# The output projection of a state-space block in high and low parts, two pieces of the FFN later

## The reference, cut to what matters

```python
xz = einsum('bld,ed->ble', layernorm(x), in_proj_w)      # 256 -> 2 x 512
x_inner, z = split(xz, 2)
x_conv = silu(causal_conv_4_taps(x_inner) + conv_b)
x_dbl  = einsum('bld,ed->ble', x_conv, x_proj_w)         # delta, B, C
y = scan(h = h * exp(delta * A) + x_conv * delta * B; y = h . C)
y = (y + x_conv * D) * silu(z)
x = x + einsum('bld,od->blo', y, out_proj_w)             # 512 -> 256, the output projection
h = gelu(butterfly(layernorm(x) @ W_exp + b_exp) + up_bias)
x = x + butterfly(h) @ W_con + b_con + down_bias         # 1024 hidden
```

## Time and profile before

| | |
|---|---|
| time, median of 3 runs (all) | 543.49 us (544.0, 543.46, 543.49) |
| profiled execution, its own time | 543.8 us |
| its span, first to last instruction | 542.1 us |
| busy in the span: TensorE, VectorE, ScalarE, GpSimd | 516.0, 416.8, 307.0, 93.3 us |
| mean granted TensorE clock | 0.981 of full speed |

### The profile page before, as it was taken

One profiled execution on the slowest core, in us unless ns is written; L12 is line 12 of the kernel. 1 busy time (PEld: TensorE's weight loads), 2 busy tenths in 40 slices (PEclk: granted clock), 3 DMA queues, 4 the chain that ended last, 5 costly groups with the idle time before them and its releaser, 6 DMA issues.

```text
span 542.1 us, 8227 instructions
## 1 busy us (share of the span) xinstructions
PE 516.0 (95%) x3012; PEld 422.5 (78%) x3012; DVE 416.8 (77%) x892; ACT 307.0 (57%) x537; POOL 93.3 (17%) x88
## 2 busy tenths in 40 slices
PE   4989999998999999999999999999999999889997
PEld 3756776776887788878888788888888789578886
DVE  4778999888984999489975999489956986576542
ACT  2777883794249622875269722964278514951242
POOL 4040200220211202140211211030213021122020
PEclk9995988999999999999999999999999999999999
DMA  9652511200112001210112002110021001200011
GB/s 223 134 28 3 83 39 41 66 16 2 39 40 76 6 2 50 69 41 1 40 40 81 0 2 79 54 28 2 0 79 42 1 1 39 81 0 1 1 40 39
DMA packets 42635, 21.75 MB, mean 40 GB/s; under 512 B 26435, under 2 KB 41027, under 8 KB 42596
## 3 DMA queue, kind: packets, MB, share of 16 engines
q1 hardware_dynamic: 39956, 17.57, 13.9%
q10 hardware_dynamic: 2640, 3.67, 2.4%
HBM read 16.78 MB, written 4.46 MB: 39 GB/s over the span
## 4 chain that ended last, share of the span: by engine, by line
PE 58%; DVE 20%; ACT 9%; issue 9%; POOL 2%; DMA 1%; DVEq 0%; ACTq 0%; POOLq 0%
PE wide L715 11%; PE acc L877 11%; PE wide L866 9%; PE wide L855 9%; DVE xc L1516 5%; PE wide L829 4%; DVE state L1621 3%; PE small L705 3%; PE wide L840 2%; ACT xc L1186 2%; DVE diag_sum L1639 2%; DVE diag L1635 2%; DVE hid_low L1533 1%; PE wide L725 1%; PE small L735 1%
## 5 line engine op out<-in xcount | busy, mean ns | idle before, releaser
L1146 ACT ACTIVATE hid_f<-wide,bias_up 128x512 f32<-128x512 f32 x64 | 43.9, 686 | 160.5 <-PE wide L866 157.5
L1516 DVE SCALAR_TENSOR_TENSOR xc<-xi,taps,xc 128x512 f32<-128x512 f32 x96 | 96.2, 1007 | 4.5 <-ACT xc L1177 2.3
L877 PE MATMUL acc<-w_down_high,hid_high 128*128 128x256 f32 x256 | 73.7, 288 | 3.5 <-DVE hid_low L1533 3.4
L877 PE MATMUL acc<-w_down_high,hid_low 128*128 128x256 f32 x256 | 72.0, 281 | 0.0
L877 PE MATMUL acc<-w_down_low,hid_high 128*128 128x256 f32 x256 | 72.0, 281 | 0.0
L1533 DVE TENSOR_TENSOR hid_low<-hid_f,hid_high 128x512 fp32r<-128x512 f32 x64 | 47.4, 743 | 15.5 <-ACT hid_high L1259 15.2
L855 PE MATMUL wide<-w_out,xc 128*128 128x256 f32 x256 | 58.4, 388 | 0.7 <-DVE xc L1660 0.5
L715 PE MATMUL wide<-xnT_ln1T_high,w_in_high 128*128 128x512 f32 x128 | 56.7, 443 | 0.0
L877 PEld LDWEIGHTS acc<-w_down_high,hid_high 128*128 128x128 f32 x256 | 48.3, 188 | 10.2 <-issue 6.6
L866 PE MATMUL wide<-xnT_ln2T_high,w_up_high 128*128 128x512 f32 x128 | 54.2, 424 | 1.7 <-DVE xnT_ln2T_low L1527 1.7
L855 PEld LDWEIGHTS wide<-w_out,xc 128*128 128x128 f32 x256 | 49.2, 194 | 7.8 <-issue 1.1
(11 more groups left out here) (193 smaller groups left out, 1035.3 us busy)
## 6 DMA issues: line engine op xcount, KB each, us to landing
x_res<-in_L_attn_x_dram SPq DMA_DIRECT2D x9, 512.0 KB, 3.5
c_near<-c_of_tokens SPq DMA_DIRECT2D x8, 512.0 KB
x_ln<-in_L_attn_x_dram SPq DMA_DIRECT2D x7, 512.0 KB, 3.6
out_dram<-x1b_xn SPq DMA_DIRECT2D x7, 512.0 KB, 2.9
xc<-in_L_attn_in_proj_w_dram ACTq DMA_DIRECT2D x2, 512.0 KB, 7.1
xc<-in_L_ffn_W_exp_dram ACTq DMA_DIRECT2D x1, 1024.0 KB, 11.1
x1b_xn<-in_L_ffn_W_con_dram ACTq DMA_DIRECT2D x1, 1024.0 KB, 15.0
raw_out<-n_L_attn_out_proj_w_dram ACTq DMA_DIRECT2D x1, 512.0 KB, 7.7
```

The costliest lines, as they stand in the source:

```text
L877: last = pe.matmul(acc[:, c, :], hid[h][:, j % HRING, c * P:(c + 1) * P], w_down[w][:, j, 0:DM], start=j == 0 and c % 2 == 0 and n == 0, s ...
L1146: ins = act.activation(out_ap, in_ap, how.pop("func"), **how)
L1516: ins = dve.scalar_tensor_tensor(xc[u % BATCH][:, e, :], xi[:, e, tap:tap + TILE], taps[:, e, tap:tap + 1], xc[u % BATCH][:, e, :], ALU.mu ...
```

## The change

`out_projection` of units 2 to 7 is made in high and low parts. The gated output is split by `high_of_gated` on ScalarE (a pair of blocks at a time, 128x1024) and `low_of_gated` on VectorE. The high part is written in the place of `z`, the low part in that of `xc`. `w_out` is split once, in phase 1, into `w_out_r`, which has the place of `con_mixed`. In phases 2 to 6 the projection moves behind `up(p, 5)` and `down(p, 3)`; in phase 7 it stays behind `down(p, 4)`. On VectorE `low_hidden(p, 5)` moves ahead of the residual in these phases. Units 0 and 1 keep the exact projection in its place. No DMA is added or moved.

```diff
-    first, between, then = (3, 0, 2) if phase < HALVES_FROM else (3, 1, 1) if phase + 1 < UNITS else (4, 1, 1)
+    first, between, then = (3, 0, 2) if phase < HALVES_FROM else (3, 1, 2) if phase + 1 < UNITS else (4, 1, 1)
...
+        y_low, y_high = ([sb(f"y_{part}{b}", [P, CB, TILE], F32R) for b in range(BATCH)] for part in ("low", "high"))
+        w_out_r = [sb(f"w_out_{part}", [P, CB, DM], F32R) for part in PARTS]
...
             def out_projection(u, h):
                 bank = tile_of("out", h, u)
                 free(pe, u, "out", h)
+                if u >= HALVES_FROM:
+                    if h == 0:
+                        pe.wait_ge(w_out_low, 1)
+                        wait(pe, y_low_ready, u - HALVES_FROM, CB // 2)
+                    y = (y_high[u % BATCH], y_low[u % BATCH])
+                    for q in range(2):
+                        for n, (g, w, x) in enumerate((g, w, x) for g in range(CB) for w, x in PASSES):
+                            last = pe.matmul(bank[:, q * DM:(q + 1) * DM], y[x][:, g, (2 * h + q) * P:(2 * h + q + 1) * P],
+                                             w_out_r[w][:, g, :], start=n == 0, stop=n == CB * len(PASSES) - 1)
+                    mark_written(last, "out", h, u)
+                    return
...
                     transposes(r, "ln1T", x_ln, norm1)
-                out_projection(u, 0)
-                out_projection(u, 1)
+                if u < HALVES_FROM:
+                    out_projection(u, 0)
+                    out_projection(u, 1)
                 up(p, 5)
                 down(p, 3)
+                if u >= HALVES_FROM:
+                    out_projection(u, 0)
+                    out_projection(u, 1)
...
+            def high_of_gated(u, pair):
+                blocks = slice(2 * pair, 2 * pair + 2)
+                wait(act, gated, u, 2 * pair + 2)
+                act.activation(y_high[u % BATCH][:, blocks, :], xc[u % BATCH][:, blocks, :], ACT.Copy)\
+                    .then_inc(y_high_ready.handle, 1)
+            def high_of_w_out():
+                for q in range(4):
+                    wait_taken(act, ("w_down", q, 0))
+                act.activation(w_out_r[0][:, :, :], w_out[:, :, :], ACT.Copy).then_inc(w_out_high, 1)
...
                 gelu(p, 3)
+                if u >= HALVES_FROM:
+                    high_of_gated(u, 0)
                 gelu(p, 4)
+                beside("gelu 4")
                 if r < UNITS:
                     high_parts(r, "ln1T")
+                if u >= HALVES_FROM:
+                    high_of_gated(u, 1)
                 gelu(p, 5)
...
+            def low_of_gated(u, pair):
+                blocks = slice(2 * pair, 2 * pair + 2)
+                wait(dve, y_high_ready, u - HALVES_FROM, pair + 1)
+                dve.tensor_tensor(y_low[u % BATCH][:, blocks, :], xc[u % BATCH][:, blocks, :],
+                                  y_high[u % BATCH][:, blocks, :].bitcast(F32), ALU.subtract).then_inc(y_low_ready.handle, 1)
...
                 gates_of_halves(u, 0)
                 low_hidden(p, 2)
+                low_of_gated(u, 0)
                 if r < UNITS:
                     first_normalise(r)
                 gates_of_halves(u, 1)
                 low_hidden(p, 3)
+                low_of_gated(u, 1)
                 convolve(v, 2)
...
             def to_last_outputs(u):
...
                 gates_of_halves(u, 0)
+                low_of_gated(u, 0)
                 low_hidden(p, 3)
                 gates_of_halves(u, 1)
+                low_of_gated(u, 1)
...
                     low_parts(r, "ln1T")
-                if v == UNITS:
+                if u >= HALVES_FROM:
                     low_hidden(p, 5)
                 first_residual(u, 0)
                 first_residual(u, 1)
                 second_stats(u)
-                if v < UNITS:
+                if u < HALVES_FROM:
                     low_hidden(p, 5)
                 second_normalise(u)
                 low_hidden(p, 6)
                 low_hidden(p, 7)
+                if u == 1:
+                    low_of_w_out()
```

More of the change, by code:

```diff
@@ L183, in bass_preln_ssm_butterfly_ffn @@
         halo = [sb(f"halo{b}", [P, CB, HALO]) for b in range(BATCH)]
-        xc = [sb(f"xc{b}", [P, CB, TILE]) for b in range(BATCH)]
-        z = [sb(f"z{b}", [P, CB, TILE]) for b in range(BATCH)]
+        with ExitStack() as under_gated:
+            xc, z = ([under_gated.enter_context(nc.sbuf_tensor(f"{name}{b}", [P, CB, TILE], F32)) for b in range(BATCH)]
+                     for name in ("xc", "z"))
+            con_mixed = under_gated.enter_context(nc.sbuf_tensor("con_mixed", [P, HB, DM], F32))
+        y_low, y_high = ([sb(f"y_{part}{b}", [P, CB, TILE], F32R) for b in range(BATCH)] for part in ("low", "high"))
+        w_out_r = [sb(f"w_out_{part}", [P, CB, DM], F32R) for part in PARTS]
         x_tok = sb("x_tok", [P, GR, DI])
@@ L310, in bass_preln_ssm_butterfly_ffn @@
         gated = Signal(sem("gated"), CB)
+        y_high_ready = Signal(sem("y_high_ready"), CB // 2)
+        y_low_ready = Signal(sem("y_low_ready"), CB // 2)
+        w_out_high = sem("w_out_high")
+        w_out_low = sem("w_out_low")
         x1b_ready = Signal(sem("x1b_ready"), 1)
@@ L344, in bass_preln_ssm_butterfly_ffn @@
         raw_con = x1b_xn2[:, :, :, :].rearrange("p a b d -> p (a b) d")
-        con_mixed = sb("con_mixed", [P, HB, DM])
         high_w = [sb(f"high_w{i}", [P, HIGH, HB // 2, 4]) for i in range(2)]
@@ L1368, in weights_of_ffn @@
                     prepare(17)
+                elif place == "gelu 4":
+                    high_of_w_out()
             prepare(0)
@@ L1683, in gates_of_halves, with low_of_w_out @@
                     dve.tensor_tensor(own[:, g, :], own[:, g, :], z[u % BATCH][:, g, :], ALU.mult).then_inc(gated.handle, 1)
+            def low_of_gated(u, pair):
[3 more added lines that the diff above has]
+                                  y_high[u % BATCH][:, blocks, :].bitcast(F32), ALU.subtract).then_inc(y_low_ready.handle, 1)
+            def low_of_w_out():
+                dve.wait_ge(w_out_high, 1)
+                dve.tensor_tensor(w_out_r[1][:, :, :], w_out[:, :, :], w_out_r[0][:, :, :].bitcast(F32), ALU.subtract)\
+                    .then_inc(w_out_low, 1)
             def first_residual(u, h):
```

## The result

The changed kernel takes **563.56 us** (median of 4 runs, 562.16 to 564.76), the kernel before 543.48 beside it: a ratio of **1.0362**, 95% interval 1.0348 to 1.0377. It is slower by 20 us. The forecast was 558.4, with a range of 550 to 564; the time lies at the top of that range, not in its middle, and two of the four runs are above it.

What follows compares the result with a forecast made beforehand. TensorE and VectorE were taken to bound the kernel side by side from the gates to `down(p, 6)`. Losses of 12.0 (units 2 to 5), 0.3 (unit 6) and 2.3 (unit 7) on 543.8 gave 558.4 us, range 550 to 564.

Steps and rivals of the forecast that it cites:

- VectorE's queue is as long as TensorE's up to `down(p, 6)`: From the gates to `down(p, 6)`, VectorE's work and waits last as long as TensorE's, to 0.1 us.
- The middle unit: Units 2 to 5: VectorE delays of 1.80, 1.15 and 0.23 less about 0.2 give 3.0 us a unit, 12.0 in all.
- The 0.2 that was to come back: Middle units: the wait at `down(p, 6)` takes the detour over GELU 7, table load and SiLUs off the path, about 0.2 us.
- GpSimd's hold: Second difference stands still until GpSimd's residual addition is done; without it a middle unit gains 1.45 us.
- The product: TensorE's 48 products of high and low parts take 5.64 us where the exact product took 6.91; gain 1.1 a unit.
- Unit 6: First difference fits VectorE's idle 2.14 us, the second ends after TensorE wants it: +0.3 us.
- E + 15.5: Unit 6: old time of `down(p, 6)`, 458.0, counted from the second gates' end (E), said to use unit 3's offsets.
- Unit 7: Low part 4 comes 3.6 us late behind the second difference, the projection gives back 1.3: +2.3 us.
- The clock: Rival: TensorE's clock falls to half in the new waits, 6.5 us a unit, 584.4, or 565 if once; chance 0.05.
- TensorE as the bound: Rival: VectorE's idle time is usable, 6 x 1.1 us are gained, time 537.2; chance 0.04.
- GpSimd not in the way: Rival: GpSimd doesn't hold the second difference, which ends at 2.45 us behind the gates; time 550.3; chance 0.12.
- A further wait that I hadn't seen: Rival: slower copies or a further wait in units 6 and 7, up to 1.3 us more a unit, 565; chance 0.12.

Runs made afterwards that it cites:

- run 2: Changed kernel without VectorE's two differences of y, the low-part pass reading the high part (output lacks y's low part): 541.86 us, 0.997 of the kernel before.
- run 4: Changed kernel with GpSimd's addition early, differences ahead of low part 3, projection ahead of `down(p, 3)`, low parts of `ln1T` and last convolution moved: 541.33 us, ratio 0.9956.
- run 5: Kernel before the change, exact product kept, with GpSimd's residual addition moved early alone: 543.53 us, ratio 1.0.
- run 6: Kernel before the change, exact product kept, with GpSimd's addition early and low parts of `ln1T` and last convolution moved: 544.04 us, ratio 1.0012.
- run 3: Changed kernel with `up(p, 7)` made twice in phases 2 to 6, same result: 560.66 us, ratio 1.0317 to the kernel before.
- run 1: Changed kernel with GpSimd's residual addition moved to when VectorE has summed the diagonal (unit 7: states ready): 552.36 us, ratio 1.017 to the kernel before.
- run 7: Changed kernel with GpSimd's addition early and low parts of `ln1T` and last convolution moved, differences and projection left in place: 545.58 us, ratio 1.004.
- run 10: Changed kernel with GpSimd's addition early and `up(p, 7)` made twice in phases 2 to 6: 550.67 us, ratio 1.013 to the kernel before.

## Why the prediction was right, and where it was short

- **The finding that carried it, that VectorE's queue is as long as TensorE's up to `down(p, 6)`, is shown.** Without the differences TensorE waits there all the same (run 2), with VectorE relieved and the places changed it doesn't and the change becomes a gain (run 4), and with VectorE relieved but the exact product kept there is no gain (runs 5 and 6): both queues were full.
- **The middle unit was right to 0.1 us.** Forecast 3.0, measured 62.50 - 59.57 = 2.9 with the clock up (run 3), 2.96 in unit 3 of the changed kernel. Step by step: `first_normalise` 1.75 later (forecast 1.80); the second difference ends 3.93 us behind the gates' end (274.30 for 269.08 + 1.29 = 270.37), forecast 3.9; wait ahead of the projection 1.75 (1.9), at `down(p, 6)` 1.73 (2.1); GpSimd's power for the second norm, with low part 5 no longer beside it, 1.02 us (1.01). From low part 2 to low part 6 it is 287.07 - 263.65 = 23.42 us for 279.33 - 259.08 = 20.25, so 3.2 later, as forecast. The 0.2 that was to come back does: low part 2 stands 35.33 us behind the unit's `x_projection` (228.32) for 35.54 (223.54).
- **GpSimd's hold** was forecast at 1.45 a unit; taking it away gave back 62.5 - 61.0 = 1.5 (run 1). In unit 3 as in unit 7 the difference ends 1.1 us behind GpSimd's addition. The Trainium skill (SBUF — State Buffer, Who interferes with whom) says that a VectorE instruction with two SBUF inputs and a GpSimd instruction that reads SBUF exclude each other for the whole instruction; the rows agree, 2.80 for 1.22 us, and in unit 7, where nothing of VectorE's ran when GpSimd started, 2.39 (GpSimd from 514.54 to 516.89, the difference to 517.98).
- **The product** was sized a little low: 48 take 5.82 us (274.44 to `up(p, 6)` at 280.26), forecast 5.64. It changes nothing in the middle units, where the wait takes it up. TensorE's busy time in a middle unit falls by 58.99 - 57.88 = 1.1 us in run 2, as the forecast has it.
- **Unit 6** cost 0.9 for 0.3: 0.2 is the product, and `x_projection` at its start took 2.20 us for 1.87, still at the low clock. The rest isn't assigned. The "E + 15.5" in the prediction isn't unit 3's offset, which is 280.09 - 264.08 = 16.0; the trace of before has `down(p, 6)` of unit 6 at 458.04, so the 458.0 that the sum uses is right all the same.
- **Unit 7** cost 3.5 for 2.3. Its own mechanism is as forecast: the second difference ends at 517.98, 3.5 behind E. But the wait for low part 4 is 4.03 us long, and the work behind it runs at low clock. In the chain of the changed kernel:

```profile
515.59 2.39 DVE y_low L1731
517.98 0.61 DVE hid_low L1575
518.59 0.04 issue
518.63 2.93 PE acc L895 x12
521.56 5.89 PE wide L864 x48
```

  The 12 products of `down(p, 4)` take 2.93 us. Before the change:

```profile
498.05 1.67 PE acc L877 x12
```

  In the five profiled executions with such a wait in unit 7 (2.9 or 4.0 us) the clock fell four times: in the changed kernel and in runs 3, 7 and 10, and not in run 1.
- **The clock is the step that failed**: it was held to be a rival with a chance of 0.05 and 6.5 us a unit, and nothing of it was in the sum. A clock below 1.00 was one of the prediction's own signs of being wrong. It came, in three of four middle units and in unit 7, but short: 4.64 - 3.12 = 1.5 us in unit 2. With 1.55 + 1.55 + 1.2 in the middle units (over the 62.50 of run 3), 0.3 at the start of unit 6 and 1.3 in unit 7 it makes 5.9 us; 558.4 + 5.9 = 564.3, where the profiled execution took 564.8. So it is partly luck that the median, 563.56, lies within the range up to 564: the sum has 558.4, and two of the four runs are above 564. My argument was that waits of 2 us are milder than the case that had fallen. That was wrong: 1.7 us are enough at times. The Trainium skill (TensorE: Matmul & The Clock Gate, What's actually happening) has the full clock as something that steady work must earn; the trace agrees in direction, runs 3 and 10 show it by adding work. Why the clock falls behind the waits of units 2, 4 and 5 and not behind that of unit 3, of the same length and behind the same work, isn't settled. It may also be why the changed kernel's runs spread over 2.6 us; that isn't shown. Its two runs above 564 have the lowest mean clock (0.973 and 0.970, for 0.976 in the other two), but in run 1 the longest run (554.73) has a mean clock of 0.981, as high as any there.
- **The rivals.** TensorE as the bound: refuted by run 2. GpSimd not in the way: refuted by run 1. A further wait that I hadn't seen: none came up.

## What to carry to other kernels

A busy share of 99% on one engine doesn't say that the others are free: read, for each wait that the change will shorten, when the other engine's last input is ready now. Here it was ready 0.1 us before it was needed, so a saving on TensorE that costs VectorE 2.4 us lost, until pieces that weren't due there were moved out of that stretch, the difference and the projection changed places with others, and a SiLU was split. Even then 0.6 of the 1.1 us a unit came out (59.33 to 58.71). And price a new wait of the matrix engine twice: by its length, and by the clock behind it.

## What was not expected of the hardware

Twice, more work made a kernel faster: 1.40 us of products, made again in front of a wait of 1.7 us, lowered the time by 2.9 us (563.56 to 560.66) and by 1.7 us (552.36 to 550.67). The stretches at low clock behind the waits were short and cost 1.2 to 1.6 us each; by the starts of the products it is 0.21 us from one to the next there, 0.12 before.
